# A three-stage decoder layer: weight loads of the last stage placed ten slots later, and matmuls that wait product by product

## What is computed

```python
def _qdot(x, w, out_dtype=BF16):
    return jnp.dot(x.astype(E4M3), w.astype(E4M3), preferred_element_type=out_dtype)
ff_gate = _qdot(x, w_gating[0])
gate_value = jax.nn.gelu(ff_gate)
ff1 = _qdot(x, w_gating[1])
activations = gate_value * ff1
outputs = _qdot(activations, w_linear)
...
x = _layernorm(x + _L0_attn_ref(x, ...), axis=-1)
x = _layernorm(x + _L0_xattn_ref(x, ctx_2048, ...), axis=-1)
x = _layernorm(x + _L0_ffn_ref(x, L0_ffn_w_gating, L0_ffn_w_linear), axis=-1)
```

## Time and profile before

| | us |
|---|---|
| median of 3 runs | 1992.28 |
| lowest, highest | 1986.72, 2000.29 |
| profiled execution | 1990.09 |
| its span | 1988.2 |
| TensorE busy in it | 1899.9 |
| VectorE busy | 1497.7 |
| ScalarE busy | 1124.4 |

### The profile page before, as it was taken

The page is one execution under the profiler, slowest core; times in us unless marked ns, Lnnn a source line. Parts: engine busy times, 40 slices in busy tenths (PEclk is TensorE's granted clock), DMA queues, the critical chain, the costliest instruction groups (busy, mean ns, idle before and its releaser), DMA issues.

```text
span 1988.2 us, 31816 instructions
## 1 busy us (share of the span) xinstructions
PE 1899.9 (96%) x11460; PEld 1058.5 (53%) x11460; DVE 1497.7 (75%) x2632; ACT 1124.4 (57%) x2117; POOL 983.0 (49%) x968
## 2 busy tenths in 40 slices
PE   7999999999999888899999999999999899999997
PEld 4677777777777544344444444444444334444443
DVE  3566666666675656788888888888888639999997
ACT  3345444444444425688888888888888673333230
POOL 3455546555465422344444444444444137666664
PEclk9999999999999868999999999999999899999999
DMA  5665565555645411333443343434332500111111
GB/s 166 175 164 142 147 162 133 158 140 142 169 121 163 143 54 47 102 118 119 126 126 112 108 119 119 119 116 117 104 110 91 183 29 16 43 43 43 64 43 43
DMA packets 149900, 220.56 MB, mean 111 GB/s; under 512 B 41848, under 2 KB 50552, under 8 KB 149000
## 3 DMA queue, kind: packets, MB, share of 16 engines
q1 hardware_dynamic: 140078, 216.96, 37.8%
q10 hardware_dynamic: 9664, 1.58, 0.5%
HBM read 83.95 MB, written 32.02 MB: 58 GB/s over the span
## 4 chain that ended last, share of the span: by engine, by line
PE 65%; DVE 14%; DMA 7%; POOL 5%; SPq 3%; issue 3%; ACT 2%; ACTq 0%; DVEq 0%; POOLq 0%
PE bank L1282 9%; PE bank L1317 8%; PE bank L1611 8%; PE bank L85 7%; PE bank L86 6%; PE bank L87 6%; PE bank L1325 5%; PE bank L1587 5%; PE bank L572 4%; DMA xa_den<-inv 3%; PE bank L626 3%; DVE sa_mneg L698 2%; PE bank L639 2%; DVE xa_mneg L1360 2%; DVE sa_xnat L712 2%
## 5 line engine op out<-in xcount | busy, mean ns | idle before, releaser
L1360 DVE TENSOR_REDUCE xa_mneg<-bank 128x1 f32<-128x512 f32 x1024 | 646.5, 683 | 155.3 <-PE bank L1325 153.8
L1181 ACT ACTIVATE xa_prob<-bank 128x512 f32<-128x512 f32 x1024 | 549.2, 605 | 85.9 <-PE bank L1317 82.1
L1325 PE MATMUL bank<-xa_kst,xa_qst 48*128 48x512 f32 x1024 | 389.6, 462 | 21.5 <-DVE xa_mneg L1360 11.1
L1317 PE MATMUL bank<-xa_qst,xa_kst 49*128 49x512 f32 x1024 | 364.6, 442 | 14.5 <-ACT xa_prob L1181 14.3
L463 ACT ACTIVATE sa_prob<-bank 128x512 f32<-128x512 f32 x256 | 152.3, 599 | 335.7 <-PE bank L626 334.9
L1317 PEld LDWEIGHTS bank<-xa_qst,xa_kst 49*128 49x128 f32 x1024 | 166.2, 186 | 298.5 <-ACT xa_prob L1181 243.4
L1282 PE MATMUL bank<-xa_prob,xa_v 128*32 128x512 f32 x2048 | 275.6, 610 | 0.0
L1519 POOL TENSOR_TENSOR ff_total<-ff_prod,ff_mag 128x512 f32<-128x512 bf16 x128 | 194.5, 1519 | 96.1 <-DVE ff_mag L1635 96.1
L1325 PEld LDWEIGHTS bank<-xa_kst,xa_qst 48*128 48x128 f32 x1024 | 166.0, 188 | 68.7 <-DVE xa_mneg L1360 49.6
L698 DVE TENSOR_REDUCE sa_mneg<-bank 128x2 f32<-128x512 f32 x256 | 164.0, 682 | 36.2 <-PE bank L639 36.1
L1563 ACT ACTIVATE ff_gelu<-bank 128x512 bf16<-128x512 f32 x128 | 75.8, 593 | 156.6 <-PE bank L1611 156.6
(11 more groups left out here) (191 smaller groups left out, 3601.9 us busy)
## 6 DMA issues: line engine op xcount, KB each, us to landing
xa_qst<-xa_part_q SPq DMA_DIRECT2D x192, 128.0 KB, 3.6
xa_kst<-xa_part_k SPq DMA_DIRECT2D x192, 128.0 KB, 2.8
sa_qst<-sa_part_qh SPq DMA_DIRECT2D x64, 256.0 KB, 4.1
sa_kst<-sa_part_kh SPq DMA_DIRECT2D x64, 256.0 KB, 5.4
xa_den<-inv SPq DMA_DIRECT2D x64, 256.0 KB
sa_xraw<-xT SPq DMA_DIRECT2D x32, 256.0 KB, 4.1
sa_qst<-sa_part_ql SPq DMA_DIRECT2D x32, 256.0 KB, 4.1
sa_kst<-sa_part_kl SPq DMA_DIRECT2D x32, 256.0 KB, 6.0
```

Of the source, the lines that this page charges most:

```text
L1181: act.activation(prob[place[e]][:, :], banks[eb[e]][:, :], ACT.Exp, scale=X_SCALE)\
L1317: pe.matmul(banks[eb[e]][:, :], kst[u % 3][rows_of, head // 2, t * P:(t + 1) * P], qst[u % 3][rows_of, head // 2, :], start=True, stop=Tru ...
L1325: pe.matmul(banks[mb[m]][:, :], qst[u % 3][rows_of, n // 8, t * P:(t + 1) * P], kst[u % 3][rows_of, n // 8, :], start=True, stop=True).the ...
L1360: dve.tensor_reduce(mneg[:, u % 2, column:column + 1], banks[mb[m]][:, :], AX.X, ALU.max, negate=True).then_inc(s_mfree, 1)
```

## The change

Two edits. The first turn of the feed-forward stage comes behind slot 1032 of cross-attention and no longer behind slot 1022. In `down`, the wait for all sixteen rounded products of a pass ahead of the loop becomes a wait in front of each of the sixteen matmuls, for its own product.

```diff
             wait.wait_ge(s_wo, 16)
-            wait.wait_ge(s_hq, HT * (p + 1))
             wait.wait_ge(s_sum, n - 1)
             if n < 2:
                 left.bank(wait, (7, 2)[n])
             for h in range(HT):
+                wait.wait_ge(s_hq, HT * p + h + 1)
                 last = pe.matmul(lb[n % 2][:, :], hq[p % 2][:, h, t * P:(t + 1) * P],
                                  wo[:, h, :], start=(h == 0), stop=(h == HT - 1))
...
-FFN_AT = [1022, 1046, 1070, 1078, 1086, 1094, 1108]
+FFN_AT = [1032, 1046, 1070, 1078, 1086, 1094, 1108]
```

## The result

| | before | changed |
|---|---|---|
| median of 14 runs, us | 1992.34 | 1982.23 |
| lowest, highest | 1986.72, 2000.29 | 1975.02, 1988.24 |
| span of the profiled execution | 1988.2 | 1981.8 |

The ratio of the changed kernel to the one before is 0.9940, with a 95% interval of 0.9927 to 0.9953: 9 to 15 us less, 12 by the ratio and 10 by the medians. The prediction was 1982.0, in a range of 1975 to 1990.

The account below looks back on a forecast made before the run. TensorE was taken to bound the kernel, with gains only where it stands: 1990.1 - 4.2 - 4.9 = 1981.0, leaned towards the three runs' median to 1982. Range 1979 to 1985 at 0.6, 1975 to 1990 for 8 in 10.

Parts of the forecast that it names:

- the second hole at slot 1044: Cross-attention: TensorE stands again for about 4.4 us from 1561.0, waiting for the maxima row or VectorE, and resumes at 1565.4.
- What stands behind these 4 MB on SyncE's queue waits for them: SyncE's DMA queue: any DMA behind the loads waits for them, whatever its size; the 2 MB load needs 12.5 us to land.
- The first rival: Cross-attention: small DMAs pass the loads, no second hole, 10.4 and 4.9 us won, 1976; chance 0.05.
- signs of being wrong: Small DMAs landing before the 2 MB load, first tile over 3.45 us, clock 0.5 behind last products, span above 1986 without both waits.
- First edit, 4.2 us: Cross-attention, slot 1032: loads ten slots later remove the 8.77 us wait for `xa_kst`; 4.2 us won, bounds 10.4 won to 2 lost.
- the term of the half clock: Slots 1033 to 1044: 0.4 us taken off 8.3; 4.4 us won instead of 6.3 if the clock falls again in the hole.
- the denominator chain: SyncE, halves 58 and 59: the chain moves up by 4.2 us only, not TensorE's 6.3, and ScalarE takes TensorE with it.
- Second edit, 4.9 us: Tail, last linear matmuls: end at 1977.5 instead of 1982.46, 3.0 us from matmuls in the hole and 1.9 from the clock.
- the hole only moved: Rival, cross-attention: the chain of halves 58 and 59 comes as late as the stack piece, first edit gives about 0, 1986; chance 0.12.
- the half clock kept in the tail: Rival, tail: the clock stays at half, 3.0 us won instead of 4.9, 1984; chance 0.13.
- the slower one by waits: Rival, seven woven passes: 105 waits keep weight loads from being fetched ahead, 0.12 us each, 13 us, 1995; chance 0.08.
- the accumulation held back until all products are there: Rival, linear matmuls: the engine holds the accumulation back, so the second edit doesn't do what it says, 1987; chance 0.02.

## Why the prediction was right, point by point

**What stood, and what takes the hole's place.** Right, place by place: the second hole at slot 1044, VectorE at the reciprocal of half 58. Counted from slot 1031, which the two profiles reach 1.7 us apart, TensorE was to resume 14.0 us later and did so after 14.5 (1564.21 against 1549.75). The hole was put at 4.4 us and measured 4.7, 3.1, 3.4 and 3.3 in the four profiles of the changed kernel and 3.3 with the loads alone; VectorE's wait was put at some 6 and measured 5.1. One further profile of the changed kernel shows what I had listed as a sign of being wrong, a span above 1986 (1988.3) with both waits gone; it had 34 us of half clock.

**The reading that carried it.** Here the prediction was right for a reason that didn't hold. "What stands behind these 4 MB on SyncE's queue waits for them": the run with the loads on ScalarE's queue shows the same lateness. The rows of the kernel before could not tell the two apart, because all that was late there stood on one queue too. The row of 11.2 us for 8 KB shows that a small DMA is late, not why. The first rival, small DMAs that pass the loads, falls as a forecast, though not to the letter: the sums were there for VectorE at 1562.43 and the first DMA of the row landed at 1562.5, 1.4 and 1.3 us before the 2 MB load ahead of them. That order was on my list of signs of being wrong. It freed nothing, because the row's second DMA, which TensorE needs too, landed at 1564.2.

**First edit, 4.2 us.** Too small. The runs give 8.4 (6 to 11), the profiles' means 6.3. The step that failed is the term of the half clock: I took 0.4 us for it between slots 1033 and 1044 and put nothing behind that. The profile that I worked from had the shortest of four such stretches, 14 us at half clock against 24, 38 and 37. Right behind the old hole, from TensorE's resuming to slot 1046, the half clock went on for 3.9 us in it and for 10.3, 8.7 and 11.6 in the three others; behind the new hole it was 3.0 to 3.7 us in all five profiles with the loads at 1032 on SyncE's queue. So slots 1031 to 1046 are 7.0 us shorter in the mean (23.9 against 16.9), where the two first profiles differ by 4.4. At equal half clock over the whole stretch the edit is worth 4.4 us, near the 4.2 summed; the rest is that the shorter hole is in the mean followed by less half clock (23 us against 28, which at 0.36 is 2 us).

That 4.2 had another reason: of TensorE's 6.3 us the denominator chain was to take back 2. This can't be seen. VectorE waited 0 to 0.65 us at half 59 in the five profiles with the loads at 1032 and 0 to 0.47 in the four with them at 1022, and slots 1046 to 1107 take 51.9 us in the mean against 51.2, less than the scatter. I call this term open.

**Second edit, 4.9 us.** Right to a tenth, in all steps: 14 matmuls in the hole, full clock behind it, 10.8 us from the last product to the last matmul, 0 for 105 waits. The even 0.216 us across the waits of L1611 was the right row for their price, the 0.34 us of the f32 pair the wrong one.

**The sum and the lean.** 1981.0 and one more for the scatter gave 1982 against 1982.23. Two errors met in it: the first edit is worth 2 to 4 us more than I said, and the profiled execution of before was a favourable one. That the sum came out to a quarter of a microsecond is therefore luck; the range would have held either error alone. The rivals: the hole only moved (no: 4.4 us are gained at slot 1046 even in the pair of profiles that show no gain at slot 1107), the half clock kept in the tail (no, 0.216 us from matmul to matmul), the slower one by waits (no), the accumulation held back until all products are there (no, fourteen of its matmuls run ahead).

## What to carry to other kernels

A big load hurts in the moments when small DMAs with a waiter behind them are under way, on whatever queue: list those for the load's whole time to land, here 12 to 13.5 us or 16 to 18 slots, and put it where none has a waiter, or cut it to what their slack covers. Moving it by ten slots only exchanged the stack piece for the maxima row; moving it by five more cost over half of the gain, and past the last row it gave, with the new waits, 18 to 20 us in all. Where an in-order engine waits for a group of inputs at the end of a chain, a wait per input lets it work on those that are there, and here 105 such waits cost nothing that can be seen.

A single profile is a poor base for a term that hangs on the clock: compare several, by a stretch between two counted instructions.

## What the runs showed of the hardware

The stretches of half clock behind a hole are not the hole's alone. In the first profile of the changed kernel the granted clock fell to 0.5 again at 1597, 33 us after TensorE had resumed, and stayed there for 20 us. TensorE had waited for 0.5 us at the longest since 1570, and in the 7.4 us before the fall ScalarE, whose exps follow TensorE's products, was busy for 7.3. In all five profiles with the loads at 1032 on SyncE's queue this fall came 33 to 34 us after the hole, in the four with the loads at 1022 it came 26 to 55 us after it (at 1616, for 3 us, in the first), and with the loads late, where there was no hole at all, it came at 1604 and 1612 in the two profiles, for 7 us each. How long the clock stays down differs between executions of one program. The Trainium skill in "TensorE: Matmul & The Clock Gate" (What's actually happening) says that the number of matmuls at the low clock is run-variable at a kernel's start; the rows show it in the middle of one. I had taken the clock to follow the hole, and had priced it by one.

An 8 KB DMA took 1.8 to 2 us with the engines free. Beside the 4 MB those of the maxima row took 8.6 to 10.1 us on the same queue and 5.8 and 10.2 on another, the reciprocal store 10.4 to 11.5 on the same, and the sums 10.1 to 10.6 us on the same queue and 11.8 on another until VectorE could use them.
